# Four graph layers and four feed-forward layers in one program: the first graph layers' attention product computed already transposed

## What is computed

```python
x = x + L0_gnn(ln(x)); x = x + L0_ffn(ln(x)); x = x + L1_gnn(ln(x)); x = x + L1_ffn(ln(x))
x = x + L2_gnn(ln(x)); x = x + L2_ffn(ln(x)); x = x + L3_gnn(ln(x)); x = x + L3_ffn(ln(x))
```

```python
h = (x @ W1).reshape(n, H, C)
alpha = softmax over the incoming edges of leaky_relu(a_src[src] + a_dst[dst])
out = segment_sum(h[src] * alpha[:, :, None], dst) + b1     # per head: attention matrix times h
y = activation(out)                                         # ELU in L0 and L3, ReLU in L1
second attention layer on y @ W2, one head of 768 channels, + b2
```

## Time and profile before

| | |
|---|---|
| median of 3 runs | 1194.94 us (1194.56 to 1195.54) |
| profiled execution | span 1192.7 us from first to last instruction; the time around it is not recorded, the median is 2.2 us above |
| PE | 1138.3 us busy, 6347 matmuls |
| DVE, ACT, POOL | 581.9, 458.6, 22.4 us busy |
| DMA | 443.15 MB, mean 372 GB/s |

### The profile page before, as it was taken

How to read it: one execution, slowest core, us unless ns; L and a number is a source line. 1 busy time by engine, 2 the same in 40 slices (tenths; PEclk the granted TensorE clock), 3 DMA queues, 4 the chain that set the end, 5 groups by cost and what they waited for, 6 DMA issues and landing times.

```text
span 1192.7 us, 15701 instructions
## 1 busy us (share of the span) xinstructions
PE 1138.3 (95%) x6347; PEld 720.4 (60%) x6347; DVE 581.9 (49%) x892; ACT 458.6 (38%) x526; POOL 22.4 (2%) x48
## 2 busy tenths in 40 slices
PE   8899999999999999989999999999999999889988
PEld 6667785775855455536776686565665555445533
DVE  7877754756644334302665774454544532232410
ACT  4756624433633233201453464353434432222210
POOL 2000010000000000000000000000000000000000
PEclk9999999999999999999999999999999999999999
DMA  9998565957999999999685498999999999999997
GB/s 368 425 398 336 218 234 217 375 229 312 409 411 427 425 425 425 426 418 418 277 334 207 176 411 329 428 423 427 425 424 427 425 424 426 424 427 425 425 423 283
DMA packets 45368, 443.15 MB, mean 372 GB/s; under 512 B 5088, under 2 KB 5248, under 8 KB 11888
## 3 DMA queue, kind: packets, MB, share of 16 engines
q1 hardware_dynamic: 42336, 427.05, 86.5%
q0 software_dynamic: 2960, 15.09, 3.3%
HBM read 441.73 MB, written 0.39 MB: 371 GB/s over the span
## 4 chain that ended last, share of the span: by engine, by line
PE 75%; DMA 15%; DVE 4%; SPq 3%; ACT 3%; issue 1%; DVEq 0%; POOL 0%
PE PJ L2091 14%; PE PJ L2060 10%; PE AC L2128 8%; PE TP L2150 7%; DMA ring<-in_weights 7%; DMA scratch<-in_weights 6%; PE PJ L2069 5%; PE AC L1853 3%; DMA extra<-in_weights 3%; SPq L648 2%; PE AC L1840 2%; PE MS L1641 2%; PE PJ L2051 2%; PE TP L2101 2%; PE PJ L1774 1%; PE TP L2019 1%
## 5 line engine op out<-in xcount | busy, mean ns | idle before, releaser
L2091 PE MATMUL PJ<-ring,picked 128*64 128x512 f32 (+1 forms) x588 | 149.7, 594 | 0.0
L918 ACT ACTIVATE low<-PJ 128x512 f32<-128x512 f32 x51 | 30.2, 592 | 239.0 <-PE PJ L2091 168.8
L1398 DVE SCALAR_TENSOR_TENSOR act<-low,CB,PJ 128x512 f32<-128x512 f32 x51 | 38.0, 744 | 159.1 <-PE PJ L2060 82.1
L2091 PE MATMUL PJ<-scratch,picked 128*32 128x512 f32 (+1 forms) x360 | 108.6, 599 | 2.2 <-DMA extra<-in_weights 2.2
L2150 PE MATMUL TP<-ring,extra 128*64 128x512 f32 (+3 forms) x384 | 101.9, 488 | 2.8 <-issue 2.8
L1416 DVE TENSOR_TENSOR ring_lo<-ring,w_lo_u 128x1536 fp32r<-128x1536 f32 x40 | 69.2, 1754 | 54.1 <-ACT w_lo_u L935 54.1
L2150 PE MATMUL TP<-scratch,extra 128*64 128x512 f32 (+3 forms) x320 | 85.9, 488 | 0.4 <-DMA ring<-in_weights 0.4
L935 ACT ACTIVATE w_lo_u<-ring 128x1536 fp32r<-128x1536 f32 x40 | 58.1, 1485 | 68.1 <-DMA ring<-in_weights 31.5
L2091 PEld LDWEIGHTS PJ<-ring,picked 128*64 128x64 f32 (+1 forms) x588 | 42.7, 124 | 55.6 <-issue 54.9
L1416 DVE TENSOR_TENSOR ring_lo<-ring,w_hi_u 128x1536 fp32r<-128x1536 f32 x34 | 58.9, 1755 | 24.7 <-ACT w_hi_u L935 24.3
L935 ACT ACTIVATE w_hi_u<-scratch 128x1536 fp32r<-128x1536 f32 x26 | 37.5, 1482 | 76.5 <-DMA scratch<-in_weights 60.6
(11 more groups left out here) (469 smaller groups left out, 2253.6 us busy)
## 6 DMA issues: line engine op xcount, KB each, us to landing
ring<-in_weights SPq DMA_DIRECT2D x147, 1536.0 KB, 17.8
scratch<-in_weights SPq DMA_DIRECT2D x73, 1536.0 KB, 21.1
extra<-in_weights SPq DMA_DIRECT2D x39, 1536.0 KB, 22.7
extra<-in_attn POOLq DMA_DIRECT2D x11, 768.0 KB, 10.4
ring<-in_weights SPq DMA_DIRECT2D x8, 768.0 KB, 29.7
extra<-in_attn POOLq DMA_DIRECT2D x6, 512.0 KB, 10.6
extra<-in_weights SPq DMA_DIRECT2D x4, 768.0 KB, 25.5
ring<-in_weights SPq DMA_DIRECT2D x8, 384.0 KB, 16.9
```

The costliest lines, as they stand in the source:

```text
L918: A(silu, PJ[:, 0:SEG], ACT.Silu).then_inc(S("silu_ready"), 1)
L1398: v.scalar_tensor_tensor(hexp, silu, weight, PJ[:, SEG:2 * SEG], ALU.mult, ALU.mult) \
L2091: ins = mm(dst[c], x[:, t, c], slab_at(LOAD[q, kind, side])[:, t * SEG:(t + 1) * SEG], start=(t == 0), stop=(t == KT - 1))
```

## The change

The attention product is computed turned. h is now stationary, 128 channels at a time, and the attention matrix moves (128 columns), so channels are on the partitions of the result and each segment is four matmuls (eight instructions). They go where the turned segment went, MS or TP (`turned_bank`), and the activation is applied there. Bias: its rows are laid out as 128 columns of four rows each, so `rows_split` (now 2*64 partitions) is the stationary side and four repeated columns of `pick` move. The turns and their copies from PSUM are gone. In their place ACT copies the high part from the activated segment in SBUF (`segment_hi`), or in c = 2 directly from PSUM with the ReLU; plain float32 products read `act1` itself. DVE's low parts read `act1` instead of PSUM (in c = 2 PSUM, with the max). `act1T` is gone. Waits follow: attend i waits for activation i-2, `activate` for the low part or the product that read its buffer two segments before, the product for low part or activation.

```diff
 FIRST = {
-    0: dict(slab=0, segs=12, per=3, bias=0, elu=True),
-    2: dict(slab=32, segs=2, per=1, bias=12, elu=False),
-    5: dict(slab=119, segs=4, per=1, bias=14, elu=True),
+    0: dict(slab=0, segs=12, per=3, bias=(0, 0), elu=True),
+    2: dict(slab=32, segs=2, per=1, bias=(1, 0), elu=False),
+    5: dict(slab=119, segs=4, per=1, bias=(1, 8), elu=True),
 }
-LAYER2_BIAS = {1: 18, 3: 19, 6: 20}
-ROW_BV, ROW_BF2, ROW_MIXED = 21, 22, 23
-ROWS = 32
+LAYER2_BIAS = {1: 48, 3: 49, 6: 50}
+ROW_BV, ROW_BF2, ROW_MIXED = 51, 52, 53
+ROWS = 64
 FFN0_SLAB = 24
...
 SEG_BASE = {0: 0, 2: 12, 5: 14}
+ELU_BASE = {0: 0, 5: 12}
 GROUP_BASE = [0, 4, 5, 7, 8, 11, 15]
...
-def copied(c, i):
+def made(c, i):
...
         return "segmentTl_ready", sum(is_split(0, j) for j in range(i + 1))
+    if c == 2:
+        return "graphTl_ready", i + 1
     if c == 5 and graph_split(i):
         return "graphTl_ready", FIRST[2]["segs"] + i - 1
-    return "segmentT_ready", SEG_BASE[c] + i + 1
+    return "segment_ready", ELU_BASE[c] + i + 1
+def plain(c, i):
+    return made(c, i)[0] == "segment_ready"
+def high_copies(c, i):
+    return sum(not plain(b, j) for b in (0, 2, 5) for j in range(FIRST[b]["segs"]) if (b, j) <= (c, i))
...
             return PJ[:, (j % 2) * SEG:(j % 2 + 1) * SEG]
+        def turned_bank(i):
+            return MS[:] if i % 2 == 0 else TP[:, 0:SEG]
...
                 if FIRST[c]["elu"]:
-                    e = {0: 0, 5: 12}[c] + i
+                    e = ELU_BASE[c] + i
                     act.wait_ge(S("segment_product"), SEG_BASE[c] + i + 1)
                     if i >= 2:
-                        act.wait_ge(S("segment_ready"), SEG_BASE[c] + i - 1)
-                    A(low[i % 2], bank(i), ACT.Relu, scale=-1.0).then_inc(S("low_ready"), 1)
+                        act.wait_ge(S("segment_ready"), e - 1)
+                    A(low[i % 2], turned_bank(i), ACT.Relu, scale=-1.0).then_inc(S("low_ready"), 1)
                     act.wait_ge(S("low_ready"), e + 1)
...
-            def segment_turned(c, i):
-                s = SEG_BASE[c] + i
-                act.wait_ge(S("segment_turned"), s + 1)
+            def segment_hi(c, i):
+                if plain(c, i):
+                    return
+                if FIRST[c]["elu"]:
+                    act.wait_ge(S("segment_ready"), ELU_BASE[c] + i + 1)
+                else:
+                    act.wait_ge(S("segment_product"), SEG_BASE[c] + i + 1)
                 if i >= 2:
...
                     act.wait_ge(S(name), value)
-                dst = act1Th if is_split(c, i) or c == 2 or c == 5 and graph_split(i) else act1T
-                A(dst[:, i % 2, :], MS[:] if i % 2 == 0 else TP[:, 0:SEG], ACT.Copy) \
-                    .then_inc(S("segmentT_ready"), 1)
+                if FIRST[c]["elu"]:
+                    ins = A(act1Th[:, i % 2, :], act1[i % 2], ACT.Copy)
+                else:
+                    ins = A(act1Th[:, i % 2, :], turned_bank(i), ACT.Relu)
+                ins.then_inc(S("segment_hi"), 1)
...
                         low_exp(c, first + 1)
-                        segment_turned(c, first)
+                        segment_hi(c, first)
                         low_exp(c, first + 2)
-                        segment_turned(c, first + 1)
+                        segment_hi(c, first + 1)
                         split_hi(w2_slab(c, first + 1))
-                        segment_turned(c, first + 2)
+                        segment_hi(c, first + 2)
                         if g == groups:
...
                         graph_split_hi(3, (1,))
-                    if 0 <= t - 3:
-                        segment_turned(c, t - 3)
+                    if c == 5 and 0 <= t - 3:
+                        segment_hi(c, t - 3)
                     if 0 <= t - 2 < n:
...
                         low_exp(c, t - 2)
+                    if c == 2 and 0 <= t - 2 < n:
+                        segment_hi(c, t - 2)
                     if c == 5 and 2 <= t < 4:
...
-                s = SEG_BASE[c] + i
-                z = bank(i)
-                dve.wait_ge(S("segment_product"), s + 1)
+                dve.wait_ge(S("segment_product"), SEG_BASE[c] + i + 1)
                 if i >= 2:
-                    dve.wait_ge(S("segment_turned"), s - 1)
-                if FIRST[c]["elu"]:
-                    dve.wait_ge(S("low_exp"), {0: 0, 5: 12}[c] + i + 1)
-                    v.scalar_tensor_tensor(act1[i % 2], low[i % 2], -1.0, z, ALU.add, ALU.max) \
-                        .then_inc(S("segment_ready"), 1)
-                else:
-                    v.tensor_scalar(act1[i % 2], z, 0.0, None, ALU.max).then_inc(S("segment_ready"), 1)
+                    name, value = multiplied(c, i - 2) if plain(c, i - 2) else made(c, i - 2)
+                    dve.wait_ge(S(name), value)
+                dve.wait_ge(S("low_exp"), ELU_BASE[c] + i + 1)
+                v.scalar_tensor_tensor(act1[i % 2], low[i % 2], -1.0, turned_bank(i), ALU.add, ALU.max) \
+                    .then_inc(S("segment_ready"), 1)
...
-                dve.wait_ge(S("segmentT_ready"), SEG_BASE[2] + i + 1)
-                v.tensor_tensor(act1Tl[:, i % 2, :], MS[:] if i % 2 == 0 else TP[:, 0:SEG],
-                                act1Th[:, i % 2, :].bitcast(F32), ALU.subtract).then_inc(S("graphTl_ready"), 1)
+                dve.wait_ge(S("segment_hi"), high_copies(2, i))
+                v.scalar_tensor_tensor(act1Tl[:, i % 2, :], turned_bank(i), 0.0, act1Th[:, i % 2, :].bitcast(F32),
+                                       ALU.max, ALU.subtract).then_inc(S("graphTl_ready"), 1)
...
-                dve.wait_ge(S("segmentT_ready"), SEG_BASE[c] + i + 1)
-                v.tensor_tensor(act1Tl[:, i % 2, :], MS[:] if i % 2 == 0 else TP[:, 0:SEG],
-                                act1Th[:, i % 2, :].bitcast(F32), ALU.subtract).then_inc(S("segmentTl_ready"), 1)
+                dve.wait_ge(S("segment_hi"), high_copies(c, i))
+                v.tensor_tensor(act1Tl[:, i % 2, :], act1[i % 2], act1Th[:, i % 2, :].bitcast(F32),
+                                ALU.subtract).then_inc(S("segmentTl_ready"), 1)
...
-                f, C, s = FIRST[c], GAT[c]["C"], SEG_BASE[c] + i
-                bias_row(bank(i), f["bias"] + i, 0, SEG, start=True)
+                f, C, dst = FIRST[c], GAT[c]["C"], turned_bank(i)
+                block, row = f["bias"][0], f["bias"][1] + 4 * i
+                mm(dst.rearrange("p (t n) -> p t n", t=4), rows_split[:, block * P:(block + 1) * P],
+                   pick[:, row:row + 4].unsqueeze(2).to_broadcast([2 * ROWS, 4, P]), start=True, stop=False,
+                   skip_group_check=True)
                 if c == 0:
...
                     pe.wait_ge(S("attn_ready"), GROUP_BASE[c] + i + 1)
-                at = i * SEG
-                while at < (i + 1) * SEG:
-                    h = at // C
-                    end = min((h + 1) * C, (i + 1) * SEG)
-                    g = h // GAT[c]["group"]
-                    a = group_at(c, g) + (h % GAT[c]["group"]) * P
-                    o = at - i * SEG
-                    ins = mm(bank(i)[:, o:o + end - at], attn_tile(c)[:, a:a + P], h_tile(c, i)[:, o:o + end - at],
-                             start=False, stop=(end == (i + 1) * SEG), skip_group_check=True)
-                    at = end
+                for t in range(4):
+                    h = (i * SEG + t * P) // C
+                    a = group_at(c, h // GAT[c]["group"]) + (h % GAT[c]["group"]) * P
+                    ins = mm(dst[:, t * P:(t + 1) * P], h_tile(c, i)[:, t * P:(t + 1) * P],
+                             attn_tile(c)[:, a:a + P], start=False, stop=True, skip_group_check=True)
                 ins.then_inc(S("segment_product"), 1)
...
-            def turn_segment(c, i):
-                s = SEG_BASE[c] + i
-                pe.wait_ge(S("segment_ready"), s + 1)
-                if i >= 2:
-                    name, value = copied(c, i - 2)
+            def product2(c, j, between=lambda t: None):
+                n, last = w2_slab(c, j), FIRST[c]["segs"] - 1
+                if c != 2:
+                    name, value = made(c, j)
                     pe.wait_ge(S(name), value)
-                dst = MS if i % 2 == 0 else TP
-                for t in range(4):
-                    ins = nc.tensor.transpose(dst[:, t * P:(t + 1) * P], act1[i % 2][:, t * P:(t + 1) * P], ident[:])
-                ins.then_inc(S("segment_turned"), 1)
-            def product2(c, j, between=lambda t: None):
-                n, last = w2_slab(c, j), FIRST[c]["segs"] - 1
-                name, value = copied(c, j)
-                pe.wait_ge(S(name), value)
                 xh, xl = act1Th[:, j % 2, :], act1Tl[:, j % 2, :]
...
+                    pe.wait_ge(S("segment_hi"), high_copies(2, j))
                     pe.wait_ge(S("graph_lo"), 2 * (2 + j) + 1)
...
                         for a, b in halves():
```

(28 more changed lines are left out.)

14 lines of the change are left out of this document (5 added, 9 removed).

## The result

The changed kernel takes 1180.27 us (median of 4 runs, 1178.03 to 1183.24) beside 1195.24 us for the kernel before on the same chip (4 runs, 1194.56 to 1197.25): ratio 0.9896, 95% interval 0.9872 to 0.992. By the medians the change is faster by 15.0 us in this pair (the ratio gives 12.4) and by 11.6 to 13.5 us in later ones. The profiled execution spans 1181.4 us (before 1192.7).

What follows compares the result with a forecast made beforehand. The prediction took PE's own order to bound the graph layers and transfers the mixtures; 1.9 + 1.15 + 1.9 - 0.45 = 4.5 us faster, off the 1194.94 us median, gave 1190.4 us, range 1186.8 to 1194.3.

Steps and rivals of the forecast that it cites:

- Bias: Bias matmul per segment, now 128 instead of 64 rows: no cost taken, bounds 0 and 0.50 us each.
- Loads: Opening loads: the rows matrix grows to 128 rows, delaying the awaited slab; cost 0.45 us, bounds 0 and 0.5.
- Attention product: Each segment's attention product in the turned form: 0.1 us shorter, bounds 0 and 0.14.
- First layer: First graph layer: turns vanish but two new waits precede products 0 and 1; gain 1.9 us, bounds 0 and 6.9.
- Third layer: Third layer, two segments: one ACT copy replaces activation, turn and copy; gain 1.15 us, bounds 0.4 and 1.9.
- Fourth layer: Fourth layer, four segments: turns leave and attention products shorten; gain 1.9 us, bounds 1.4 and 2.6.
- The pass-through assumption: Time saved in a graph layer before a mixture moves its transfers forward and reaches the end whole.
- (1): Rival: nothing takes the turns' place, first layer gains 6.9 us; 10.3 us in all, 1184.7 us; chance 0.06.
- (2): Rival: in the first layer activation 1 comes late beside the high copy; total gain 3.0, 1191.9 us; chance 0.12.
- (3): Rival: the mixtures keep most of the gain, a quarter to a half of 4.5 left; 1193.4 us; chance 0.14.
- (4): Rival: new idle stretches per first-layer group drop PE's granted clock; 3.1 us slower, 1198.0 us; chance 0.08.
- (5): Rival: added weight loads show in 12 one-head segments; 9.3 us slower, 1204.2 us; chance 0.04.

Runs made afterwards that it cites:

- b_rows128: Kernel before with only the bias rows array enlarged, so bias matmuls contract over 128 partitions instead of 64: 1184.04 us, ratio 0.9923.
- a_again: The changed kernel rerun unchanged, for its spread and a second trace: 1183.28 us, ratio 0.9901 to the kernel before.
- a_base3: The changed kernel rerun unchanged, as the measure for the 64-row and 96-row bias variants on the same chip: 1181.05 us, ratio 0.9887.
- b_load128: Kernel before with the 128-row load and the tiles behind the pick matrix 128 bytes further, bias matmuls still over 64 rows: 1190.02 us, ratio 0.9973.
- a_hi64: Changed kernel with its bias matmuls taking only rows 1 to 64, memory and loads unchanged: 1187.97 us, ratio 0.9944 to the kernel before.
- experiment 3: Changed kernel with bias matmuls cut to 64 or 96 rows: 1187.97 and 1182.47 us, beside 1181.05 us for the changed kernel unchanged.
- b_sbuf: Kernel before with only the pick matrix widened, so all tiles behind it lie 128 bytes further in SBUF: 1190.47 us, ratio 0.9974.
- b_narrow: Kernel before with its attention product cut into four matmuls of 128 columns per segment, old form and turns kept: 1194.99 us, ratio 1.0007.
- a_turns: Changed kernel with 72 identity transposes put back at the turns' old places, results unread: 1182.43 us, ratio 0.9895 to the kernel before.
- a_base4: The changed kernel rerun unchanged, as the measure for a tile-placement and an instruction-order variant: 1180.38 us, ratio 0.9882.

## Why the prediction was wrong

**The ledger.** Of the 13.5 us between the medians of the last pair, the place of tiles gives 3.0 to 3.6, the rows of the bias matmul 6.0 to 6.9, the turned product the rest, 3 to 4.5. The forecast knew only the last. Single medians of one kernel move by 1 to 3 us, so these are sizes, not exact shares. The last share is the least certain: on one chip b_rows128 and the changed kernel (a_again) differ by 0.8 us of medians, 2.6 by the ratios (0.9923, 0.9901), across chips by 4.3 (a_base3), and the intervals overlap. It rests on the stages of the profiles. The best bounds that the prediction gave the three layers, with the load at nothing, come to 11.4 us, 1183.5: no choice within its turns' terms reaches the result.

- **The failed step: "Bias ... I take 0; bounds 0 and 0.50 us each".** It was given a cost or nothing, and never a gain. The form changes from 64 to 128 rows, and the prediction compared the matmul's own duration, not what stands between it and its neighbours. It measured -0.39 us from product to product. Between b_load128 and b_rows128 that is 1.3 + 1.2 + 1.0 = 3.5 us in the graph layers, between a_hi64 and a_base3 1.5 + 1.3 + 1.1 = 3.9. Not all of 0.39 a segment arrives: three segments of a group in the first layer could save 1.2 us, and the group gets 0.3 us shorter (34.4 to 34.1 us from product 0 to product 0); one thing that takes it is the wait for activation 0, which grows from 0.65 to 1.05. Of the other 2 to 3 us of the medians, the second pair's may be the clock (experiment 3). In the first pair the granted clocks are alike (0.9935 and 0.9942 on average, an estimated 0.8 us), and the rest stays open: the mixtures have bias rows too, and stages that vary more than that.
- **Loads.** Cost 0.45 forecast; the opening became 0.9 us shorter, the end shows neither. Priced as bytes at the mean rate, which isn't how this load behaved. And the wider pick matrix wasn't priced at all, though it moved everything behind it by 128 bytes: 3.0 us (b_sbuf).
- **Attention product, 0.1 us shorter: not so.** With 128 rows in both, the wide form follows itself after 1.09 us and the turned one after 1.11. The 1.05 us that I compared with 0.91 held the delay of the 64-row bias load behind it; the 0.91 stood ahead of a product, with no such load. What came is the lower bound, 0. The issue-gap rule of the Trainium skill ("TensorE: Matmul & The Clock Gate", section Back-to-back issue gap), which spoke against the change, has no support in b_narrow: 4.6 us by it, at most 3.7 by the interval of the ratio.
- **First layer, forecast 1.9.** From b_rows128 to a_base3 1.1 us: right in mechanism, less in size. Both new waits appeared, 0.38 and 0.46 us instead of 0.7 and 0.6. The start of product 1, forecast 10.1 and measured 9.91, was near by luck: the turns' part of the gain is 0.28 us where 0.39 was forecast, the rows' part 0.31.
- **Third layer, forecast 1.15.** The second and third layers together gained 1.4 (102.8 to 101.4). The copy stood behind the exps as forecast.
- **Fourth layer, forecast 1.9.** 2.3 (49.8 to 47.5), of which the turns' own time is 1.8 (a_turns). The forecast's 0.2 for four shorter attends (0.4 by its own 0.1 each) had nothing behind it.
- **The sum of the three** was 4.95; these stages give 4.8. So the turns' forecast was right for the graph layers of a kernel that already has the 128 rows; that all of it reaches the end isn't shown.
- **The pass-through assumption** held through the first mixtures (337.4 us in b_rows128, 337.6 in a_base3, 337.7 in a_base4). Through the last ones it can't be told: 535.7 against 537.9 and 536.0 us, so that 4.7 and 4.4 us at the fourth layer's end are 2.5 and 4.1 at the end of the span.
- **Rivals.** (1) fell: nothing else taking the turns' place would have given 6.9 in the first layer, and product 0 waits. Its number, 1184.7, was the nearest, for another reason: luck. (2) didn't show: activation 1 started at 48.09, 0.10 us behind the end of its exp (47.36 for 0.63), although the high copy ran beside it. (3) fell with the table for the first mixtures. (4) fell: clock 1.00 from 35.6 to 154.9. (5) fell with b_narrow.

## What to carry to other kernels

Look at the weight loads of short contractions before pricing them. Here a load of 64 rows started only as the product before it ended, after 0.76 us of an idle PEld between busy matmuls, and cost 0.39 us each time; padding with zero rows to 128 took it away. When a change resizes a small tile, everything allocated behind it moves; run the kernel before with that resize alone, or the change gets the credit. And give each edit of form a bound on the side of a gain too.

## What the runs showed of the hardware that I had not expected

- A weight load of 64 rows takes 182 ns (186 to 192 for 96 or 128 rows), but it wasn't taken ahead of a running matmul of 128 rows, nor the next 128-row load ahead of the 64-row matmul's end: 1.48 to 1.51 us from product to product in seven kernels with 64 rows, 1.09 to 1.12 in six with 96 or 128. The Trainium skill, "TensorE: Matmul & The Clock Gate", section LDWEIGHTS (loading the stationary operand), says that a load's time follows from its columns and not its rows; the durations agree. The same page, section The mechanism, says that a load is taken ahead of running matmuls if its row group is free or it goes to the background buffer. Loads of 96 and 128 rows were taken ahead in these traces; no run here shows it for 64 rows, and none shows which of the two conditions applied.
- 128 bytes of shift in SBUF change the rate of the weight stream from 425 to 427 or 428 GB/s, and 256 bytes don't; 3.0 us in the kernel before (b_sbuf).
- 48 transposes in the first layer, some in places where PE would wait anyway, cost nothing (110.4 against 110.6 us); in the fourth layer, where it doesn't wait for the turned segments, 16 of them cost 1.8 us, 0.45 a turn, as the earlier trace rows has it (0.43).
